# Pad rows with a register load each, a spare pad block written later, and a slot table split around a shared unit

## The reference

```python
x = x + 0.5 * ffn(layernorm(x))
x = x + attn(layernorm(x))        # gated linear attention, 16 heads of 16
x = x + 0.5 * ffn(layernorm(x))

def ffn(x):                       # 8 experts of width 176, the best 2 per token, and a shared expert of 352
    probs = softmax(x @ gate_w.T)
    weights, indices = top_k(probs, 2);  weights /= weights.sum(-1)
    combine = (weights[:, :, None] * one_hot(indices, 8)).sum(1)
    h = silu(x @ w_gate[e]) * (x @ w_up[e])                  # for each expert e
    out = sum_e combine[:, e] * (h @ w_down[e])
    sh = (silu(x @ shw_gate) * (x @ shw_up)) @ shw_down
    return out + sigmoid(x @ shgate_w)[:, None] * sh
```

## Time and profile before

| | us |
|---|---|
| median of three runs | 933.3 (929.79 to 934.92) |
| the profiled execution | 929.79 |
| its span | 928.0 |
| TensorE matmul busy | 858.3 (92%) |
| TensorE weight load busy | 750.3 (81%) |
| VectorE busy | 612.7 (66%) |
| ScalarE busy | 526.0 (57%) |
| GpSimd busy | 468.6 (50%) |

### The profile page before, as it was taken

How to read it: one execution, slowest core, us unless ns; L and a number is a source line. 1 busy time by engine, 2 the same in 40 slices (tenths; PEclk the granted TensorE clock), 3 DMA queues, 4 the chain that set the end, 5 groups by cost and what they waited for, 6 DMA issues and landing times.

```text
span 928.0 us, 26608 instructions
## 1 busy us (share of the span) xinstructions
PE 858.3 (92%) x8334; PEld 750.3 (81%) x8334; DVE 612.7 (66%) x2096; ACT 526.0 (57%) x1548; POOL 468.6 (50%) x621
## 2 busy tenths in 40 slices
PE   4897898999999978999998999998898999999998
PEld 4786687999999966777776777776787999999997
DVE  5764555777777446776867868675464777777432
ACT  4453321666666467778768776665422666666311
POOL 4465552444444434574676767674531444444441
PEclk9988799999999989999999999999998999999999
DMA  7622244444443542132122111112334444443699
GB/s 226 186 95 91 87 141 132 121 124 131 128 127 110 134 67 41 25 47 48 33 74 71 36 48 36 71 59 71 131 111 120 146 132 127 133 133 104 123 204 248
DMA packets 70261, 99.07 MB, mean 107 GB/s; under 512 B 9120, under 2 KB 58528, under 8 KB 69856
## 3 DMA queue, kind: packets, MB, share of 16 engines
q0 software_dynamic: 29120, 51.36, 21.7%
q1 hardware_dynamic: 41008, 46.01, 17.3%
HBM read 53.36 MB, written 46.23 MB: 107 GB/s over the span
## 4 chain that ended last, share of the span: by engine, by line
PE 81%; DVE 6%; issue 6%; ACT 4%; DVEq 1%; POOL 1%; DMA 0%; SPq 0%; ACTq 0%; POOLq 0%
PE PSA L1601 15%; PE PSA L1653 15%; PE PSA L1615 9%; PE PSA L1709 7%; PE PSA L1671 5%; PE PSA L1729 3%; PE PSA L1661 3%; PE PSA L1636 3%; PE PSA L1778 3%; PE PSA L1557 3%; PE PSA L1763 2%; PE PSA L1807 2%; PE PSA L1672 2%; PE PSA L1673 2%; PE PSA L1573 2%
## 5 line engine op out<-in xcount | busy, mean ns | idle before, releaser
L1033 POOL DMA_INDIRECT expert_out<-MEM,DEST x142 | 136.2, 959 | 166.6 <-ACT MEM L1222 163.3
L1601 PE MATMUL PSA<-MEMR,SGUh 128*128 128x256 f32 (+1 forms) x768 | 173.9, 309 | 13.0 <-issue 8.4
L1653 PE MATMUL PSA<-EGUh,MEMR 128*128 x568 | 173.1, 346 | 4.9 <-DVE MEMR L1442 3.4
L1017 POOL DMA_INDIRECT expert_in<-MEM,POSU x112 | 113.8, 1016 | 64.3 <-issue 28.2
L1601 PEld LDWEIGHTS PSA<-MEMR,SGUh 128*128 128x128 f32 (+1 forms) x768 | 127.7, 191 | 22.3 <-issue 17.0
L1601 PE MATMUL PSA<-MEMR,SGUl 128*128 128x256 f32 (+1 forms) x384 | 111.6, 291 | 3.0 <-issue 2.7
L1653 PEld LDWEIGHTS PSA<-EGUh,MEMR 128*128 128x128 f32 x568 | 102.6, 187 | 10.2 <-issue 8.3
L1653 PE MATMUL PSA<-EGUl,MEMR 128*128 x284 | 91.7, 323 | 0.0
L1442 DVE TENSOR_TENSOR MEMR<-PSA,MEMR 128x256 fp32r<-128x256 f32 x142 | 60.3, 425 | 45.2 <-ACT MEMR L1202 44.9
L1523 DVE TENSOR_TENSOR MEM<-PSA,CN 128x1024 f32<-128x1024 f32 x64 | 77.3, 1210 | 14.9 <-PE PSA L1729 14.7
L1208 ACT ACTIVATE MEM<-PSA 128x176 f32<-128x176 f32 x142 | 45.2, 318 | 74.0 <-issue 47.4
(11 more groups left out here) (199 smaller groups left out, 2283.6 us busy)
## 6 DMA issues: line engine op xcount, KB each, us to landing
MEM<-expert_in SPq DMA_DIRECT2D x142, 129.5 KB
X<-expert_out POOLq DMA_DIRECT2D x30, 512.0 KB, 7.4
turned<-MEM SPq DMA_DIRECT2D x8, 512.0 KB
MEM<-turned SPq DMA_DIRECT2D x8, 512.0 KB, 3.5
out<-X SPq DMA_DIRECT2D x16, 256.0 KB, 4.6
X<-in_L_attn_x SPq DMA_DIRECT2D x7, 512.0 KB, 6.6
expert_out<-MEM,DEST POOLq DMA_INDIRECT x142
expert_in<-in_pads SPq DMA_DIRECT2D x17, 129.5 KB
```

Of the source, the lines that this page charges most:

```text
L1017: pool.indirect_dma_start(out=xs_d, out_offset=bass.IndirectOffsetOnAxis(ap=POSU[:, k, i:i + 1], axis=0), in_=XN[n.xn][:, c, :], in_offset ...
L1033: pool.indirect_dma_start(out=y_d[f], out_offset=bass.IndirectOffsetOnAxis(ap=DEST[:, j:j + 1], axis=0), in_=YS[j % YSD], in_offset=None). ...
L1601: last = mm(t[0:h, w * HALF:(w + 1) * HALF], SGU[b][:, w, k, j * P:j * P + h], XT[slot][a][:, k, hf * HALF:(hf + 1) * HALF], start=i == 0, ...
L1653: last = mm(t[:, 0:2 * HE], XGR[j % 2][a][:, k, :], EGU[b][:, bass.ds(e, 1), k, :], start=i == 0, stop=i == 3 * KD - 1)
```

## The change

Three edits:

- `table` puts a shared unit between the two parts of the slot table: count, unit, `spread`, unit, `lines`, and the rest. Before it was count, unit, `spread`, `lines`, units.
- SyncE reads the row number of each pad block by a load of its own just ahead of the block's DMA. Before, one load read all eight into registers. This holds for both FFNs.
- The DMA of the ninth block goes from the loading stage to behind the eight of the first FFN.

```diff
     def table(self, f, between):
         self.count(f)
-        between[0]()
-        self.slots(f, 1)
-        self.slots(f, 2)
-        for s in between[1:]:
+        for part in (1, 2):
+            for s in between[part - 1:part]:
+                s()
+            self.slots(f, part)
+        for s in between[2:]:
             s()
         self.flush()
...
-                if k == 2:
-
-                    sp.dma_start(xs_d[E * ROWS:E * ROWS + P, :].rearrange("(a b) d -> a (b d)", a=16), pad_d[E].rearrange("(a b) d -> a (b d)", a=16)).then_inc(s_padw, 16)
...
                 sp.wait_ge(s_padr, f + 1)
-                _, ends = nc.values_load_multi_w_load_instructions(PADI[0:1, 0:E], engines=[mybir.EngineType.SP], min_val=0, max_val=E * ROWS - P,
-                                                                   skip_runtime_bounds_check_because="rows that were counted")
-                for e, row in enumerate(ends):
+                for e in range(E):
+                    row = sp.value_load(PADI[0:1, e:e + 1], min_val=0, max_val=E * ROWS - P)
                     sp.dma_start(xs_d[bass.ds(row, P), :].rearrange("(a b) d -> a (b d)", a=16), pad_d[e].rearrange("(a b) d -> a (b d)", a=16)).then_inc(s_padw, 16)
+                if f == 0:
+                    sp.dma_start(xs_d[E * ROWS:E * ROWS + P, :].rearrange("(a b) d -> a (b d)", a=16), pad_d[E].rearrange("(a b) d -> a (b d)", a=16)).then_inc(s_padw, 16)
```

## The result

| | before | changed |
|---|---|---|
| median of 19 runs, us | 930.64 (926.65 to 939.29) | 936.49 (930.6 to 940.27) |
| the profiled execution | 929.79 | 936.71 |
| its span | 928.0 | 934.9 |

The ratio is 1.0054 with a 95% interval of 1.0037 to 1.0072: 5.0 us slower (3.4 to 6.7); the two medians alone are 5.85 apart, the two profiled executions 6.9. The time is inside the forecast range, and the step is several times the +1.0 of the sum.

A forecast was written before the change was run, and what follows sets the result against it. TensorE's chain was taken to bound the kernel, SyncE and VectorE counting only where they make it late. First-FFN gather delay +1.0, second FFN zero, on the 933.3 us median gave 934.3; range 928 to 940.

The forecast's parts named there:

- +1.0 of the sum: First expert tile, first FFN: TensorE delay in us, taken near the middle of 0 and 2.3; second FFN priced zero.
- forecast case: First FFN's gathers 0.8 to 4.4 us later, partly covered by slack: +0.3 to +2.3 us, chance 0.48.
- The signs: Expected at the first expert stage: first gather issued at 152.8 to 156 us, TensorE waiting at most 2 us.
- (b): Both FFNs' pads: stalls go by instruction, excess doubles, gathers 7.9 us late in the first; +7.8, 941.1 us; chance 0.20.
- Part 1: SyncE's pad rows: own load, range check and address for each, 0.80 + 0.54 = 1.34 us per pad.
- The stall: SyncE's pads, first FFN: 3.56 us lost before; ninth pad at 149.5 without it, 153.1 with all of it.
- Part 2 and 3: Before the first gathers: ninth pad DMA costs one issue, 0.56 us; later slot table, ready at 152.0, delays first gather 0.8.
- The slack: First expert tile: gather landed by 154.1, TensorE transposes it at 156.23, so 2.1 us of delay cost nothing.
- second leg: Second FFN: read of turned activations lands near 711 instead of 704, ScalarE's copy 3 us late, TensorE loses some 2.
- (a): Start of expert stage: all hidden, stalls shrink, first gather moves 0.8 us against 2.1 of slack; 933.3 us, chance 0.20.
- (c): Ahead of both expert stages: spread-out pads starve TensorE and ScalarE less; 924.7 us at best, 928.4 gaps alone; chance 0.12.
- the bound of 0.5%: Whole kernel: a measurement can tell about 0.5%, 4.7 us, from no change.

The follow-up runs named there:

- double loads: Kernel before with single pad loads, each done twice with its range check, in both FFNs, on the faster chip: ratio 1.0096 (1.0079 to 1.0112).
- grouped loads: Kernel before with eight single pad loads and range checks, all ahead of the first pad DMA, in both FFNs: ratio 1.0060 (1.0029 to 1.0090).
- the pads behind the scatters: Kernel before, but SyncE waits for all scatters ahead of the pads in the first FFN: 938.69 us, one execution.
- the kernel that holds them: Kernel with single loads, GpSimd holding the first FFN's last eight scatters until all pads have landed: 902.84 us, one execution, faster chip.
- the kernel with one load: Kernel before with the first six gathers' row numbers read by one load ahead of the waits: ratio 0.9986 on the faster chip, 0.9996 on a slower.

## Why the prediction was right, and where not

*The number.* The median of 936.5 us lies in the range of 928 to 940, and this is in part luck. The sum began from the median of three runs, 933.3, where 19 runs have 930.64: 2.7 too high. Its step of +1.0 was some 4 us too small. The two errors point opposite ways and partly cancel: 936.5 is 2.2 above the forecast of 934.3. The step of 5.0 lies outside the +0.3 to +2.3 of the forecast case. The signs fall between the cases as well: the first transpose waits 3.68 us, over the 2 of the forecast and under the 4 of (b), and the first gather goes at 159.72, after the 157 of (b), though 3.2 of that is the later count.

*What bounds the kernel.* TensorE's chain, with SyncE beside it: right. The change costs where it makes the gathers later than the last down, and on the slower chips nowhere else that the runs could tell.

*Part 1, pad pace.* 1.34 us forecast, 1.28 to 1.36 measured. The bulk pace of 0.77 was 0.78 on the chip without stalls. The Trainium skill, "Runtime: NRT & Kernel Launch", section "Instruction fetch mechanics", has about 200 ns per register for loads from HBM, even in bulk, which no run here shows. For these registers from SBUF an equal price does not hold: one load alone has a median of 0.27 us, eight in one load took 0.53 to 0.73, under 0.1 each.

*The stall.* From the count, the last pad was put at 10.7 us with no stall and 14.3 with all of the 3.56 us of before; it is 14.5, with 3.8 us of stall. The bound was nearly exact, and taking the middle was the mistake: the rows gave no reason for half. In the second FFN the excess over the undisturbed 10.2 us grew from 2.9 to 5.0, so that the last pad came 6.2 us later from the count, outside the 1.2 to 4.1 of the sum. Of the doubled stalls of rival (b), 2.9 to 5.7 us, about three quarters of the growth came there, and almost nothing in the first FFN (3.56 to 3.8).

*Part 2 and 3.* Right: ninth block and table are each covered, together too. `ROWI` was put at 13.2 us after the count and came at 13.0.

*The slack.* This term was too favourable. Its 2.1 us were read from one execution. The time from the count to the end of the downs, which sets it, was 17.6 us there and 16.3 in the profile of the changed kernel; among the other kernels with the bulk load and undelayed pads on the slower chips there are two, of five, in which TensorE already waits (1.1 and 1.5 us). In the changed kernel's profile the first gather is 5.85 us later relative to the end of the downs: 4.6 from the pads, 1.25 because the count was closer to the downs. Less 2.1 of slack that is 3.75, and 3.68 was measured.

*What was left out.* Behind the wait come costs that the sum did not have. The first product is 0.8 us later than the wait explains, which I put down to the second gather, 1.1 us behind the first, without having tested it; and the stretch at the lower clock costs about 1.1. A wait of TensorE was priced at its length; here it cost 5.6 for 3.7 (7.5 less the 1.9 by which the downs ended later). So against the +1.0 of the sum the place has 1.5 more from the stall, 1.25 from the slack and 1.9 from what was left out.

*The rivals.* (b) had the right place and threshold, gathers more than 2.1 us late, but not the reason: its doubled stalls did not come in the first FFN. What came was the upper end of the forecast's own sum, with less slack and a dearer wait: 5.0 us, where (b) had 7.8. Its second leg, the read of turned activations, was seen only with double loads. (a) would have been right only without stalls. (c) falls with the changed kernel itself, where ScalarE still stands 8.9 us and TensorE's gaps are 2.1 us instead of 2.6, and with the grouped loads and the pads behind the scatters: the gaps are there with no pad in flight (TensorE's 2.5 and 1.3 us, the latter in a single run). The ratio's interval runs on both sides of the bound of 0.5%, to which "no change" had been given 0.68.

*Still open:* why the instructions of SyncE, TensorE and ScalarE come in steps of 0.7 us in some stretches and on some chips. Not the pads; not the scatters alone. Whether the scatters have a part in it on the slower chips was not tested, since the kernel that holds them ran on the fast one. In the Trainium skill, "Runtime: NRT & Kernel Launch", section "Instruction fetch mechanics", the cost of crossing a block boundary while instructions are streamed is "mostly hidden". Executions of the same kernel at 895 and 930 us would fit a delivery of instructions that is hidden on one chip and not on the other, but no run here proves it.

## What to carry to other kernels

Count the instructions of a queue that stands ahead of a gather, not only its DMAs: here a load and two small instructions more for each of eight pads, 0.6 us a pad, were what used up the slack, and a bulk register load avoids them. Take slack from several executions, since both of its ends move. Price a wait of TensorE above its length when the rows show a lower clock behind such waits, and when a stall is measured at a place, let the sum hold also if all of it stays.

## What the runs showed of the hardware that was not expected

Two chips run the same program 35 us apart (895.4 and 930.1 to 932.0 us medians of the kernel before), and the profiles (on the faster one, of three kernels close to it) differ in one thing above all: gaps of "issue" on TensorE, 27 with 16.8 us up to 155 us on one, none over 0.3 us on the other up to the first expert product. On the slower chips single instructions of SyncE last up to 0.87 us whose medians are 0.03 to 0.27. On the faster one the first gathers wait 9.0 us for the last scatter in the kernel with one load, and the last pad with single loads is only 4.1 us later (10.8 instead of 6.7 after the count). By this estimate the change of the pads costs the first FFN something on one chip and nothing on the other; that was not timed.
